# Releasing GpSimd's gathers one by one and holding its scatters for two more edge sums in a two-layer graph kernel

## What is computed

```
def _L0_gnn_ref(x, edge_index, edge_attr, distances, ...):
    radial = _gaussian_smearing(distances)
    row, col = (edge_index[0], edge_index[1])
    edge_features = jnp.concatenate([x[row], x[col], radial], axis=-1)
    h = silu(edge_features @ Wm1 + bm1)
    h = silu(h @ Wm2 + bm2)
    messages = h @ Wm3 + bm3
    out = jax.ops.segment_sum(messages, col, num_segments=x.shape[0])
    u = silu(jnp.concatenate([x, out], axis=-1) @ Wu1 + bu1)
    u = u @ Wu2 + bu2
    u = silu(u @ Wi1 + bi1)
    return u @ Wi2 + bi2

def _L1_gnn_ref(x, adj, edge_attr, att_w, att_b):
    src, dst = (adj[0], adj[1])
    xt = logmap0(x, C)
    xs = xt[src]
    feats = jnp.concatenate([xs, xt[dst], edge_attr], axis=-1)
    adj_att = jax.nn.sigmoid(feats @ att_w.T + att_b)
    agg_add = jax.ops.segment_sum(xs * adj_att, src, num_segments=N)
    mean_src = jax.ops.segment_sum(edge_attr, src, num_segments=N) / cnt_src
    mean_dst = jax.ops.segment_sum(edge_attr, dst, num_segments=N) / cnt_dst
    support_t = xt + agg_add + mean_src + mean_dst
    return proj(expmap0(support_t, C), C)

x = _layernorm(x + _L0_gnn_ref(x, [src, dst], edge_attr_16, edge_weight, ...))
x = _layernorm(x + _L1_gnn_ref(x, [src, dst], edge_attr_128, ...))
```

## Time and profile before

| | |
|---|---|
| three timed runs | 2124.50, 2124.54 and 2126.67 us, median 2124.54 |
| span of the profiled execution, first to last instruction | 2669.9 us |
| TensorE busy | 1766.1 us (66%) |
| VectorE busy | 1679.0 us (63%) |
| GpSimd busy | 1498.9 us (56%), 784 gathers and 784 scatters among its 1572 instructions |
| ScalarE busy | 1361.0 us (51%) |

### The profile page before, as it was taken

One profiled execution on the slowest core, in us unless ns is written; L12 is line 12 of the kernel. 1 busy time (PEld: TensorE's weight loads), 2 busy tenths in 40 slices (PEclk: granted clock), 3 DMA queues, 4 the chain that ended last, 5 costly groups with the idle time before them and its releaser, 6 DMA issues.

```text
span 2669.9 us, 41647 instructions
## 1 busy us (share of the span) xinstructions
PE 1766.1 (66%) x11127; PEld 1530.4 (57%) x11127; DVE 1679.0 (63%) x5490; ACT 1361.0 (51%) x3965; POOL 1498.9 (56%) x1572
## 2 busy tenths in 40 slices
PE   5677777777878787776643244777775666576770
PEld 5466665655666666565533233677665656576660
DVE  5666666666666677776535334788765555466668
ACT  3666665665666666875425333666643233233224
POOL 3566666665666666655566665566555455555510
PEclk8788888898888778997755556677777677777795
DMA  7465655654333233333433335566555455455541
GB/s 192 122 148 124 150 131 130 148 133 111 88 84 86 84 86 85 87 83 103 133 89 100 87 105 140 160 187 186 171 155 151 147 154 152 142 168 167 172 136 49
DMA packets 337140, 341.98 MB, mean 128 GB/s; under 512 B 67402, under 2 KB 266948, under 8 KB 336898
## 3 DMA queue, kind: packets, MB, share of 16 engines
q1 hardware_dynamic: 283474, 233.47, 33.7%
q0 software_dynamic: 50176, 104.07, 13.2%
q10 hardware_dynamic: 3248, 1.71, 0.3%
HBM read 246.14 MB, written 90.15 MB: 126 GB/s over the span
## 4 chain that ended last, share of the span: by engine, by line
PE 30%; DVE 20%; issue 17%; another core or an unknown queue 15%; ACT 11%; DVEq 3%; SPq 0%; DMA 0%; ACTq 0%
PE bank L1651 8%; PE bank L1010 5%; PE bank L1630 4%; PE bank L1311 3%; DVEq L758 3%; PE bank L1284 3%; PE bank L1324 3%; DVE rt L987 2%; ACT L1093 2%; ACT L779 2%; ACT ring L1093 1%; PE bank L1320 1%; DVE ring L1184 1%; DVE ring L978 1%
## 5 line engine op out<-in xcount | busy, mean ns | idle before, releaser
L933 POOL DMA_INDIRECT gtab<-ring,idx x784 | 753.9, 962 | 556.3 <-ACT ring L952 238.9
L1060 POOL DMA_INDIRECT ra<-ptab,gis x784 | 744.9, 950 | 491.6 <-issue 199.7
L1010 PE MATMUL bank<-ring 128*128 128x78 f32 x1568 | 299.9, 341 | 284.0 <-issue 220.9
L949 ACT ACTIVATE rt<-rt 128x254 f32<-128x254 f32 x536 | 215.4, 403 | 470.7 <-DVE rt L989 347.6
L1010 PEld LDWEIGHTS bank<-ring 128*128 128x128 f32 x1568 | 278.0, 258 | 306.6 <-issue 251.0
L1284 PEld LDWEIGHTS bank<-ring 128*128 128x128 f32 x1568 | 232.9, 215 | 175.9 <-issue 153.8
L1073 ACT ACTIVATE ring<-bank 128x512 f32<-128x512 f32 x196 | 116.3, 594 | 395.3 <-remote 349.0
L1284 PE MATMUL bank<-ring 128*128 128x78 f32 x1568 | 238.1, 293 | 103.4 <-issue 86.4
L1651 PE MATMUL bank<-ring 128*128 128x130 f32 x1312 | 230.7, 332 | 86.5 <-issue 67.2
L1630 PE MATMUL bank<-rt 128*128 128x126 f32 x1072 | 196.6, 328 | 108.0 <-issue 73.8
L1311 PEld LDWEIGHTS bank<-wm,ring 128*128 128x128 f32 x1568 | 250.7, 228 | 25.5 <-issue 10.9
(11 more groups left out here) (274 smaller groups left out, 3817.3 us busy)
## 6 DMA issues: line engine op xcount, KB each, us to landing
ring<-in_edge_attr SPq DMA_DIRECT2D x196, 256.0 KB
ring<-gtab SPq DMA_DIRECT2D x89, 393.0 KB
gtab<-ring SPq DMA_DIRECT2D x36, 687.8 KB
ra<-in_edge_weight SPq DMA_DIRECT2D x132, 128.0 KB
ring<-gtab SPq DMA_DIRECT2D x49, 327.5 KB
ring<-reld SPq DMA_DIRECT2D x196, 78.0 KB
ring<-gtab SPq DMA_DIRECT2D x49, 262.0 KB
ra<-ptab,gis POOLq DMA_INDIRECT x784
```

Of the source, the lines that this page charges most:

```text
L933: G.indirect_dma_start(out=gtab[group_of(i)][:, :], out_offset=bass.IndirectOffsetOnAxis(ap=idx[:, n, i:i + 1], axis=0), in_=row[i % NE][: ...
L949: k = S.activation(prl[i % NPR][:, n, :], prl[i % NPR][:, n, :], ACT.Identity, accum_out=lgs[i % 2][:, n:n + 1])
L1010: k = T.matmul(bk[:, 256:256 + W], row[i % NE][:, n, 0:H], od2[i % NO2][:, n, :], start=(first and n == 0), stop=(n == 3), skip_group_chec ...
L1060: G.indirect_dma_start(out=gp[i % NGP][:, n, :], out_offset=None, in_=ptab[:, :], in_offset=bass.IndirectOffsetOnAxis(ap=gis[:, n, i:i + 1 ...
```

## The change

Two waits are added on GpSimd. No instruction that does work is added, removed or moved.

- **Gathers.** The wait ahead of a chunk's four gathers becomes one wait ahead of each. With j = i - 6: the first still waits for `h1p` of chunk j. The others wait, from chunk 9 on, for three later points of TensorE's next tick: the sum of messages (`w` of chunk j-3), the ranks (`rk` of chunk j+3), and the second product (`h2p` of chunk j-1).
- **Scatters.** A chunk's first scatter waits, beside `lb`, until TensorE has summed three chunks from this one on (`rp` of at least i+3, that is chunk i+2), or all 196.

```
+AHEAD = 3
...
             e.wait_ge(s["lb"], i + 1)
+            e.wait_ge(s["rp"], min(i + AHEAD, M))
             for n in range(4):
                 G.indirect_dma_start(
...
+        def buffer_free(e, i, n):
+
+            j = i - NGP
+            if j >= 0:
+                e.wait_ge(s["h1p"], j + 1)
+                if n > 0 and j >= 3:
+                    name, v = (("w", j - 2), ("rk", j + 4), ("h2p", j))[n - 1]
+                    e.wait_ge(s[name], v)
+
         def layer_pool(e):
...
                 if i is not None:
-                    e.wait_ge(s["h1p"], i + 1 - NGP)
                     for n in range(4):
+                        buffer_free(e, i, n)
                         G.indirect_dma_start(
```

## The result

The changed kernel needs 2131.18 us (median of 8 runs, 2126.15 to 2132.89). The kernel before, run in turn with it, needs 2123.4 us (8 runs, 2121.14 to 2126.67). The ratio is 1.0027 with a 95% interval of 1.0018 to 1.0037, some 4 to 8 us more. It is slower, by a little over the 0.2% that can be told from no change. The forecast of 2125.0 us is missed by 6 us; the range of 2114 to 2141 held.

The account below looks back on a forecast made before the run. GpSimd's cadence in both stages was taken as the bound: 81 + 950 + 988 + 123 = 2142 us, against 2124.5 us timed. The change's terms, 0 + 0 + 0, gave 2125.0 us with few waits unmet; range 2114 to 2141.

Parts of the forecast that it names:

- the cover is gone: Rival, end of gathers and early stops: GpSimd has under three sums in store; 2134.6 to 2137.9 us, chance 0.32.
- The bound: Both stages: GpSimd without a pause, 1.25 us a gather and 1.26 a scatter, bounds the timed kernel; sum 2142 us.
- What the profile of before was: Whole kernel: the 2669.9 us profile was longer through TensorE's slow spells, largely the profiled execution's own; timed runs 2124.5 us.
- The waits themselves: GpSimd's instructions: 588 more gather waits and 196 scatter waits cost 0 if met; bound 4 us.
- Gathers one by one: Gathers, first stage: new waits are met 3 ticks earlier if GpSimd is the bound; value 0, bound -4.7 us.
- Scatters two sums later: Scatters: the new wait is met 3 chunks, 15 us, ahead if GpSimd is the bound; 0 to +3, bound +13.4 us.
- my own: Whole kernel: the forecast case of 2125.0 us, counted with the rival that the change does nothing; chance 0.52.
- Smoothing pays: Rival, gathers' and scatters' transfers: less in each other's way, some 8 us faster, 2116.5 us, or twice that; chance 0.16.
- What I said would show each step: Changed kernel's profile: cadence stays 1.25 and 1.26 us, scatters released by L1012, no TensorE idle ahead of L1331.
- The signs for a slower execution: Slow-state profile: span some 13 us longer, scatters two to three chunks behind sums at 2500 us, gathers' lead about 4.

Follow-up runs that it names:

- second trace: The unchanged kernel before, traced again later on the faster chip at granted clock 0.878: one run, 2119.16 us, with a traced span of 2116.5 us.
- gathers_alone: The changed kernel without the scatters' new wait, against the kernel before: ratio 0.9995 on a slower chip, 0.9999 when rerun (_2) on the faster one.
- scatters_alone: The scatters' new wait with the gathers as before, against the kernel before: ratio 0.9577 on a slower chip, 1.0034 when rerun on the faster one.

## Why the prediction was right, and where it wasn't

**The time.** The range held, but not because the step that it was built on did. The prediction said it would be wrong if the timed runs moved by over 4 us; they moved by 4 to 8. They are in the range because the rival "the cover is gone" was let into it.

**The bound.** Right. GpSimd's cadence without a pause is what bounds the kernel at 2120 us. By the second trace, the terms of the sum were 64 + 955 + 992 + 105 = 2116 us, where I had 81 + 950 + 988 + 123. The head and the tail were shorter, as I had supposed, and the two stages each 4 to 5 us longer, since the means (952, 961) stand over the 944 and 958 of a single instruction.

**What the profile of before was.** Half right. It is not a picture of the timed runs, but it need not be the profiling that brought the spells. In ordinary timed runs the kernel needs 2674 to 2705 us on two chips, at about the clock of that trace (0.761). That the trace was taken on such a chip fits, and isn't on record. "One chip or another" was not among the things I weighed.

**The waits themselves: 0.** Right, by gathers_alone_2 and by the medians; the 0.30 us between two instructions is the same with one, two or more waits. The count was a little off: since the new gather waits begin at chunk 9, they are 3 by 187 = 561 and not 588, which changes nothing.

**Gathers one by one: 0.** Right in the price and in the reason (GpSimd is behind, its waits long met); wrong in the lead. I read 4.5 chunks at 600 us off a trace in which TensorE was late. In the second trace of the kernel before, gathers begun (L1060) and blocks used (L1320) by 600 us are:

```profile
0.00:600.00 600.00, 429.53 (x451) 0.95 0.67 164
```

```profile
0.00:600.00 600.00, 71.45 (x448) 56.43 (x448) 0.95 0.67 164
```

The lead is under one chunk, and TensorE does stand ahead of its transposes for gathers: 48.0 us in 44 places before the change, 56.6 us in 50 after it, where I had foreseen none. It costs nothing, because GpSimd has no slack to give.

**Scatters two sums later: 0 to +3.** This is the step that failed: the term measures 7.0 us. It failed by its assumption that "if GpSimd is the bound, the work ahead of it is full". In the steady part that holds, with a smaller store than I had: at 1380.1 us scatters (L933) of 286/4 = 71.5 chunks are begun, and 600/8 = 75 sums (L1010) done, in the same view:

```profile
0.00:1380.10 1380.10, 274.24 (x286) 0.86 0.55 140
```

```profile
0.00:1380.10 1380.10, 131.12 (x600) 122.11 (x600) 0.86 0.55 140
```

Chunk 71 is under way. The new wait asks for 74 sums there and finds 75: one chunk to spare, some 5 us, and not three chunks or 15 us. But at the start of the scatters the store isn't full, it is just being filled. When chunk 3's first scatter begins, at 1034.04, 40/8 = 5 sums are done and the new wait asks for 6:

```profile
0.00:1034.10 1034.10, 6.46 (x40) 5.65 (x40) 0.95 0.56 140
```

The old wait, on ScalarE's weights of the chunk itself, had let it go.

**The rival "the cover is gone".** This is what happened, and it named the place ("at the end of the gathers"). Its condition ("less than three sums in store when it begins the scatters") is nearly what the traces show: three sums are done when chunk 0's scatters start (the third at 1014.1, the scatter at 1018.9, in the second trace of before), and at chunk 3 there are two. Its price was too high: 10.1 to 13.4 us was taken at the other end of the stage, where the traced GpSimd was level with the sums. Measured is 7.0 us in the trace, and 4 to 8 us in the timed runs. The right price could have been sized only by the ticks at the transition against GpSimd's 5.05 us, and in the trace at hand the sum of chunk 3 came after a wait of 17.61 us, which the execution of the result does not have. I gave this case 0.32 and my own 0.52, because the saturation of GpSimd in the mean spoke against it. A mean over two stages says nothing of the moment at which one goes over into the other.

**Smoothing pays.** Nothing of it at 2120 us. On a slower chip the scatters' half of the change gains 4.2%, 113 us where this rival had 8 to 16. It comes with fewer long iterations and not with cheaper DMAs: the medians there are 944 and 958 ns, as in the kernel before. The gathers' mean went from 952 to 955 ns and the scatters' from 961 to 965, both with their medians. The Trainium skill (SBUF — State Buffer, "SBUF: two separate sides") has VectorE and GpSimd keep each other from a shared port pair. A few stretched instructions, up to 1.2 to 1.4 us, are in each trace as in the earlier trace rows, without any trace showing whether this lock is their cause, and no placing of gathers or scatters here changed the timed runs by way of it. The most that can be in it: the gathers' mean is 955 ns in the three traces with gathers one by one and 949 to 954 in the eleven others, 1 to 6 ns by 784, and gathers_alone_2 bounds that at 2 us.

**What I said would show each step.** The cadence stayed, the scatters are released by L1012, and a little idle time of GpSimd is new: these held. The signs for a slower execution can be looked for where each half of the change ran alone on a slower chip. In gathers_alone 363 gathers are begun and 348 blocks used at 600 us, a lead of 3.75 chunks for "about 4", and TensorE never stands ahead of its transposes for a gather. In scatters_alone 739/4 = 184.75 chunks of scatters are begun and 1504/8 = 188 sums done at 2400 us, a little over three chunks behind. Both are much as I said. What failed there is the time: 13 us more by the prediction, and 113 us less measured (2591.57 for 2704.69).

## What to carry to other kernels

An engine that never pauses in its steady part can still be short of work where one stage goes over into the next: price a new wait there first, by the end of the event it asks for in the ticks just around, not by the steady store. A wait whose reach shares a ring of buffers with a loop (here 9 less the reach) is free until the loop's trip, divided by the chunks left to it, passes the bound engine's pace; from there it costs in every chunk. And ask whether the trace and the timed runs come from the same chip and clock before a lead, a store or a slack is read off it.

## What was not expected of the hardware

- The same kernel needs 2120 us on one chip (granted clock 0.88) and 2674 to 2705 us on two others (0.77). The change's wait on the sums costs 0.34% on the first and saves 4.2% on one of the others.
- On those two, TensorE needs 9 us for eight matmuls that take 1.05 us a tick earlier, released by nothing in the trace, on a program that runs on one core. In chunks 124 to 190 the iterations of 14 us and more are 10 to 16 with free scatters and none or one with scatters tied to their own sum or the one two chunks on, the cause being open.
- GpSimd's time from one indirect DMA's end to the next one's start is 0.30 to 0.31 us in 1555 of 1567 cases in the second trace of before, and the changed kernel's further waits, once met, leave it there.
